# Second attention: scores from a head's own 32 rows, two heads side by side in the array, in place of zero-padded key copies

## The chip, the core and the metric

One core of one Trainium2 chip runs the whole program. The metric is the device time of one execution in microseconds; three runs of a kernel are taken and the median counts. Lower is better.

## The reference

Input `x` has 8 batches of 256 positions and 512 channels. What matters here is the second attention, over each batch's 256 channels-as-positions with 16 heads of 32 columns:

```python
q, k, v = (proj(Wq), proj(Wk), proj(Wv))          # 16 heads, d = 32
q, k = _rope(q, k, s, d, hidden_states.dtype)
scores = einsum('bhqd,bhkd->bhqk', q, k) / sqrt(d)
scores = maximum(scores + causal, neg)
tmp_sum = sum(softmax(scores), axis=-2)           # column sums
_, topk_idx = top_k(tmp_sum, heavy_budget)        # 25 of 256 columns
scores = where(heavy_mask | band, scores, neg)
attn = einsum('bhqk,bhkd->bhqd', softmax(scores), v) @ Wo.T
x = x + attn
x = x + ffn(gru(cond, x))
...
```

A first attention comes before it, a recurrent network and a mixture of experts behind it; neither is touched.

## The kernel before

The program is written engine by engine: each of PE (matrix products), ACT (activation functions), DVE (vector operations), POOL (general processor) and SP (transfers) has a hand-written order, and semaphores tie them together. `second_attention` runs eight batches one after the other. Queries and keys lie transposed: `rot[:, 0]` holds the rotated queries and `rot[:, 1]` the rotated keys, 128 partitions by 4 groups by 256 positions, so that four heads of 32 rows share a group of partitions. For head h, `m = h // 4` is the group and `q = h % 4` its place in it, so its rows are 32q to 32q + 31.

Before, the keys of the four places were copied into `kz[:, q]` with all rows but those of place q set to zero (a product with the 0/1 column `C_HEAD + q`): q = 0 and 1 by ACT (line 679), q = 2 and 3 by DVE (line 804). A head's score product then runs over all 128 rows, since the zeros take out the other three heads.

A batch has these stages:

- First round, 16 heads. PE: `scores(b, 0, h)`, two bf16 products that write the causal mask (lines 509, 510) and two f32 score products (line 518, query rows 0 to 127 with 128 keys; line 520, query rows 128 to 255 with 256 keys). Each f32 product runs as two weight loads and two passes. The result of head h lies in PSUM bank h % 4, so PE waits until ACT has read head h - 4. DVE: two maxima per head (lines 776, 777), then the reciprocal of head h - 1 (line 783) and its copy into `rdiag` (line 814). ACT: two exponentials (lines 662, 664). After heads 6, 10, 14 and at the end PE adds up columns for four heads at a time in four 32-column tiles of the array (line 566).
- PE then makes V (line 555) and the next batch's projections (line 528), while DVE picks the heavy columns (lines 824 to 840) and turns them into `lcol` (line 843). POOL makes a diagonal for each head from it (line 449), into `NDG` buffers.
- Second round, 16 heads. PE: `scores(b, 1, h)` with three more mask products (lines 515 to 517) that need head h's diagonal; then three transposes of head h - 3 (line 594), and after heads 7, 11, 15 and at the end the product with V of four heads in four column tiles (lines 610, 613). DVE: maxima as before, then reciprocal and two scalings of head h - 1 (lines 854, 856). ACT: exponentials, a copy of the transposes of head h - 2 (line 698), and every four heads a copy of the output (line 703).
- Seam. PE: rotation products (line 539) and output projection (line 625). DVE: rotation of the next batch (lines 795 to 800), its two copies into `kz` (line 804), then four additions to x1T (line 864). The next first round's scores wait for the copies and for all four additions, because the projection uses the same PSUM banks.

Of the kernel before, what the change touches and what calls it, by code (L numbers as in the profile page):

```python
# [9 lines left out]
ALU = mybir.AluOpType  # L10
ACT = mybir.ActivationFunctionType
AX = mybir.AxisListType

P = 128
B, S, D = 8, 256, 512
KD = D // P
KS = S // P
NH = 16
DH1 = S // NH
DH2 = D // NH  # L20
HPC = P // DH2
# [25 lines left out]
C_HEAD = C_SINK + S  # L47
# [329 lines left out]
def second_attention(nc, ins, ps, cst, ident, x1T, hT, tab, weights, d_qk, d_vo, d_tab, d_xT, gru, sb, sem):  # L377
    st = ExitStack()
    with st:
        wq, wk, wv, wo = weights  # L380
        masks = sb(st, "masks", [P, 4, P], BF16)
        raw = sb(st, "raw", [P, 2, KD, S])
        rot = sb(st, "rot", [P, 2, KD, S])
        kz = sb(st, "kz", [P, HPC, KD, S])
        v = sb(st, "v", [P, KS, D])
        tmp = sb(st, "tmp", [P, KD, S])
        E = sb(st, "E", [P, NEX, P + S])
# [13 lines left out]
        dg = sb(st, "dg", [P, NDG, KS, P], BF16)  # L401
# [13 lines left out]
        a_raw = sem(st, "a_raw")  # L415
        p_rot = sem(st, "p_rot")
        v_rot = sem(st, "v_rot")
        a_kz = sem(st, "a_kz")
        v_kz = sem(st, "v_kz")
        p_v = sem(st, "p_v")  # L420
        a_v = sem(st, "a_v")
        p_s = sem(st, "p_s")
        v_m = sem(st, "v_m")
        a_e = sem(st, "a_e")
# [6 lines left out]
        g_d = sem(st, "g_d")  # L431
# [6 lines left out]
        v_x = sem(st, "v_x")  # L438

        with nc.Block() as block:  # L440
# [43 lines left out]
            def _(pe):  # L484
# [4 lines left out]

                def scores(b, r, h, more=False):  # L490

                    n = b * (2 * NH) + r * NH + h
                    bank = h % 4
                    m, q = h // HPC, h % HPC
                    if r == 0 and h < 4:
                        if h == 0:
                            pe.wait_ge(v_x, b * KD + 1)
                    else:
                        pe.wait_ge(a_e, (n - 4 + 1) * 2)
                    if r == 0 and h == 0:  # L500
                        pe.wait_ge(v_rot, b * 6 + 6)
                    if r == 0 and h < 2:
                        pe.wait_ge(a_kz, b * 2 + h + 2)
                    elif r == 0 and h < HPC:
                        pe.wait_ge(v_kz, b * 2 + h - 1)
                    if r == 1 and h == 0 and more:
                        pe.wait_ge(a_raw, b * 2 + 4)
                    kw = dict(stop=False, skip_group_check=True)
                    nc.tensor.matmul(ps[:, bank, 0:P], masks[:, 0, :], masks[:, 1, :], start=True, **kw)
                    nc.tensor.matmul(ps[:, bank, 2 * P:3 * P], masks[:, 0, :], masks[:, 1, :], start=False, **kw)  # L510
                    if r == 1:

                        pe.wait_ge(g_d, b * NH + h + 1)
                        d = dg[:, h % NDG, :, :]
                        nc.tensor.matmul(ps[:, bank, 0:P], masks[:, 2, :], d[:, 0, :], start=False, **kw)
                        nc.tensor.matmul(ps[:, bank, P:2 * P], masks[:, 3, :], d[:, 0, :], start=False, **kw)
                        nc.tensor.matmul(ps[:, bank, 2 * P:3 * P], masks[:, 2, :], d[:, 1, :], start=False, **kw)
                    nc.tensor.matmul(ps[:, bank, 0:P], rot[:, 0, m, 0:P], kz[:, q, m, 0:P],  # L518
                                     start=False, stop=True, skip_group_check=True)
                    nc.tensor.matmul(ps[:, bank, P:P + S], rot[:, 0, m, P:S], kz[:, q, m, :],  # L520
                                     start=False, stop=True, skip_group_check=True).then_inc(p_s, 1)

                def project(b):

# [19 lines left out]
                def batch(b, more):  # L544

                    for h in range(NH + AHEAD_SUMS):
                        if h < NH:
                            scores(b, 0, h)
                        if h == NH:

                            if b == 0:
                                pe.wait_ge(d_vo, 32)
                            for c in range(KS):
                                for k in range(KD):
                                    last = nc.tensor.matmul(ps[:, 6 + c, :], hT[:, k, b, c * P:(c + 1) * P], wv[:, k, :],
                                                            start=(k == 0), stop=(k == KD - 1))
                            last.then_inc(p_v, 1)
                        g = h - AHEAD_SUMS
                        if g >= 0 and g % CGS == CGS - 1:

                            g0 = g - CGS + 1
                            pe.wait_ge(v_d, b * NH + g + 1)
                            for part, (e0, e1) in enumerate(((0, P), (P, P + S))):
                                for g in range(g0, g0 + CGS):
                                    rows = (g % CGS) * CG
                                    last = nc.tensor.matmul(ps[rows:rows + CG, 4, 0:e1 - e0], rdiag[:, g, part, :],
                                                            E[:, g % NEX, e0:e1], start=(g0 == 0 and part == 0),
                                                            stop=(g0 + CGS == NH and part == 1),
                                                            tile_position=(0, rows), skip_group_check=True)
                            last.then_inc(p_c, 1)  # L570
# [4 lines left out]
                    for c in range(KS):  # L575
                        last = nc.tensor.matmul(ps[:, 5, c * P:(c + 1) * P], light[:, c * P:(c + 1) * P],
                                                ident, start=True, stop=True)
                    last.then_inc(p_l, 1)

                    for h in range(NH + AHEAD + 1):  # L580
                        if h < NH:
                            scores(b, 1, h, more)
                        g = h - AHEAD
                        if 0 <= g < NH:
# [62 lines left out]
            def _(act):  # L647
# [16 lines left out]
                    nc.scalar.activation(E[:, h % NEX, P:P + S], ps[:, bank, P:P + S], ACT.Exp,  # L664
                                         bias=nm[:, r, h, 1:2], accum_out=ls[:, r, h, 1:2]).then_inc(a_e, 1)

                act.nop().then_inc(a_kz, 1)
                act.wait_ge(d_tab, 16)
                def copy_raw(b):
                    for i in range(2):  # L670
# [3 lines left out]
                                             ACT.Copy).then_inc(a_raw, 1)  # L674

                def batch(b, more):
                    act.wait_ge(v_rot, b * 6 + 6)
                    for q in range(2):
                        nc.scalar.activation(kz[:, q, :, :].rearrange("p m s -> p (m s)"),
                                             rot[:, 1, :, :].rearrange("p m s -> p (m s)"), ACT.Copy,  # L680
                                             scale=tab[:, C_HEAD + q:C_HEAD + q + 1]).then_inc(a_kz, 1)
                    for h in range(NH):
                        exps(b, 0, h)
                    act.wait_ge(p_v, b + 2)
# [28 lines left out]
            def _(dve):  # L713
# [72 lines left out]
                def rotate(b):  # L786

                    for i, (c, s) in enumerate(((C_COSQ, C_SINQ), (C_COSK, C_SINK))):
                        dve.wait_ge(p_rot, b * 2 + i + 1)
                        if i == 0:  # L790
                            dve.wait_ge(p_s, b * 2 * NH + 1)
                            dve.wait_ge(a_kz, b * 2 + 1)
                        cos = tab[:, c:c + S].unsqueeze(1).broadcast_to((P, KD, S))
                        sin = tab[:, s:s + S].unsqueeze(1).broadcast_to((P, KD, S))
                        nc.vector.tensor_tensor(tmp[:, :, :],
# [4 lines left out]
                        nc.vector.tensor_tensor(rot[:, i, :, :], rot[:, i, :, :], tmp[:, :, :], ALU.add)\  # L800
                            .then_inc(v_rot, 1)
                        dve.wait_ge(v_rot, b * 6 + 3 * i + 3)
                    for q in range(2, HPC):
                        nc.vector.tensor_scalar(kz[:, q, :, :], rot[:, 1, :, :], tab[:, C_HEAD + q:C_HEAD + q + 1],
                                                None, ALU.mult).then_inc(v_kz, 1)

                def batch(b, more):
                    for h in range(NH + 1):
# [76 lines left out]
    return (h % CGS) * CG + h // CGS  # L885


NDG = 3
K_STEPS = 2 + 2 * (HEAVY // 8) + 5 * (HEAVY % 8)


# [877 lines left out]
```

## Time and profile before

| what | before |
|---|---|
| median of three runs (range) | 2164.16 us (2162.59 to 2166.87) |
| profiled execution, its time | 2168.39 us |
| its span, first to last instruction | 2166.6 us |
| mean granted PE clock | 0.957 |
| PE busy | 1972.8 us (91%) |
| PE weight loads busy | 1693.5 us (78%) |
| DVE busy | 1381.9 us (64%) |
| ACT busy | 897.6 us (41%) |
| POOL busy | 318.5 us (15%) |

The profile is of one execution; the busy shares are means over stages with different limits, and the largest group of all, line 1048 of the recurrent network, lies after the second attention. A stage is read from the table of stretches (busy time of each engine between two moments) and from the timeline (instructions of one engine in order of time, with the idle time before one and the instruction that ended it). Matrix products overlap in the array: the time that each shows includes its way through the array, so the pitch from one start to the next is the cost.

### The profile page before, as it was taken

What the parts mean: (1) busy time and instruction counts of PE and PEld (TensorE: products, weight loads), DVE (VectorE), ACT (ScalarE), POOL (GpSimd) and SP (SyncE); (2) the same over time, 40 slices, a digit from 0 to 9 for tenths busy, and PEclk for the clock granted to TensorE, in tenths of its full rate; (3) what the DMA queues carried; (4) which work ended last, traced back from release to release, by engine and by line L of the source; (5) the groups of instructions that cost most, each with busy time, mean ns of one, the idle gap of its engine ahead of it and who ended that gap; (6) DMA issues with size and microseconds to landing.
All of it is one profiled execution on the core that took longest, in us unless ns stands there. A gap on an engine that the chain in (4) does not pass through costs nothing.

```text
span 2166.6 us, 80653 instructions
## 1 busy us (share of the span) xinstructions
PE 1972.8 (91%) x34348; PEld 1693.5 (78%) x34348; DVE 1381.9 (64%) x5702; ACT 897.6 (41%) x2894; POOL 318.5 (15%) x471
## 2 busy tenths in 40 slices
PE   5899999999998999886899999998998998999999
PEld 3677677677676889775798898897887987988988
DVE  5565666666666155677677677677676775776763
ACT  1355455455455233343343343343443433433433
POOL 0041231242111000241110110110110100100112
PEclk9999999999999999997999999899999998998999
DMA  8000000000001611111000000000000000000000
GB/s 316 1 1 1 1 1 1 1 1 1 1 1 59 216 61 52 51 45 34 3 18 18 21 11 18 27 4 28 18 5 25 18 18 13 18 18 12 4 12 11
DMA packets 53594, 63.19 MB, mean 29 GB/s; under 512 B 7377, under 2 KB 44113, under 8 KB 52209
## 3 DMA queue, kind: packets, MB, share of 16 engines
q1 hardware_dynamic: 53232, 58.02, 7.9%
q8 instruction: 270, 4.42, 0.9%
q14 instruction: 92, 0.75, 0.1%
HBM read 42.77 MB, written 15.24 MB: 27 GB/s over the span
## 4 chain that ended last, share of the span: by engine, by line
PE 41%; DVE 9%; issue 2%; ACT 1%; DVEq 0%; ACTq 0%
PE ps L1048 22%; PE ps L1492 9%; PE ps L1470 8%; DVE hp L1122 2%; ACT nn L1063 1%; DVE dh L1111 1%; DVE dh L1117 1%; DVE hn L1101 1%; DVE hn L1103 1%; DVE hn L1095 1%; DVE hn L1098 1%; PE ps L1481 1%; DVE hp L1125 1%; DVE ns L1113 1%; DVE h L1123 0%
## 5 line engine op out<-in xcount | busy, mean ns | idle before, releaser
L1048 PEld LDWEIGHTS ps<-hp,whf 128*128 128x128 f16 x24576 | 644.7, 96 | 111.7 <-DVE hp L1125 89.9
L1048 PE MATMUL ps<-hp,whf 128*128 128x32 f16 x24576 | 660.3, 177 | 73.4 <-DVE hp L1125 67.5
L1063 ACT ACTIVATE rz<-s,sc 128x32 f32<-128x32 f32 x512 | 164.6, 322 | 402.9 <-DVE s L1092 395.6
L1470 PE MATMUL ps<-hs,w1f 128*128 128x256 f16 x2112 | 285.4, 281 | 34.5 <-DVE wi L1671 34.5
L1492 PE MATMUL ps<-wi,w2f 128*128 128x256 f16 x2112 | 276.5, 279 | 0.0
L1591 POOL TENSOR_TENSOR wi<-wi 128x256 f16<-128x256 f32 x176 | 120.4, 689 | 1035.7 <-ACT wi L1571 1035.7
L1470 PEld LDWEIGHTS ps<-hs,w1f 128*128 128x128 f16 x2112 | 208.7, 101 | 72.3 <-DVE wi L1671 40.4
L1492 PEld LDWEIGHTS ps<-wi,w2f 128*128 128x128 f16 x2112 | 195.3, 99 | 27.2 <-issue 3.0
L1090 DVE TENSOR_TENSOR s<-ps,gi 128x32 f32<-128x32 f32 x256 | 48.6, 190 | 232.4 <-PE ps L1048 232.0
L1063 ACT ACTIVATE nn<-hn,sc 128x32 f32<-128x32 f32 x256 | 82.3, 322 | 240.8 <-DVE hn L1103 240.8
L1222 PE MATMUL ps<-x1T,wi 128*128 128x256 f32 x768 | 179.3, 391 | 1.0 <-PEq L440 1.0
L1222 PEld LDWEIGHTS ps<-x1T,wi 128*128 128x128 f32 x768 | 147.4, 196 | 20.9 <-issue 1.4
L520 PE MATMUL ps<-kz,rot 128*128 128x256 f32 x512 | 157.8, 391 | 0.0
L449 POOL TENSOR_TENSOR dg<-masks,lcol 128x256 bf16<-128x256 bf16 x128 | 78.1, 616 | 533.0 <-DVE lcol L843 454.2
L662 ACT ACTIVATE E<-ps,nm 128x128 f32<-128x128 f32 x256 | 94.4, 369 | 80.6 <-DVE nm L777 74.3
L1077 ACT ACTIVATE hs<-hp 128x64 f16<-128x64 f16 x256 | 65.0, 254 | 135.1 <-DVE hp L1125 134.7
L664 ACT ACTIVATE E<-ps,nm 128x256 f32<-128x256 f32 x256 | 120.3, 470 | 0.0
L528 PE MATMUL ps<-hT,wi 128*128 128x256 f32 x512 | 114.7, 385 | 4.8 <-PEq L273 4.8
L518 PE MATMUL ps<-kz,rot 128*128 128x128 f32 x512 | 115.8, 309 | 0.0
L528 PEld LDWEIGHTS ps<-hT,wi 128*128 128x128 f32 x512 | 98.1, 193 | 21.2 <-issue 7.7
L776 DVE TENSOR_REDUCE nm<-ps 128x1 f32<-128x128 f32 x256 | 73.3, 286 | 52.7 <-PE ps L520 50.4
L777 DVE TENSOR_REDUCE nm<-ps 128x1 f32<-128x256 f32 x256 | 105.6, 412 | 0.0
(213 smaller groups left out, 3002.5 us busy)
## 6 DMA issues: line engine op xcount, KB each, us to landing
gi_d<-stage SPq DMA_DIRECT2D x84, 128.0 KB, 1.7
gi<-gi_d SPq DMA_DIRECT2D x14, 768.0 KB, 5.1
w1f<-in_w1T SPq DMA_DIRECT2D x4, 1408.0 KB, 10.3
xall<-in_x SPq DMA_DIRECT2D x4, 1024.0 KB, 9.3
x1T<-in_xT SPq DMA_DIRECT2D x1, 4096.0 KB, 16.1
w2f<-in_w2T SPq DMA_DIRECT2D x16, 256.0 KB, 3.3
out<-x1T SPq DMA_DIRECT2D x8, 512.0 KB, 2.9
whf<-in_W_hh SPq DMA_DIRECT2D x1, 3072.0 KB, 22.4
```

What stands on the lines that cost most here:

```text
L518: nc.tensor.matmul(ps[:, bank, 0:P], rot[:, 0, m, 0:P], kz[:, q, m, 0:P], start=False, stop=True, skip_group_check=True)
L520: nc.tensor.matmul(ps[:, bank, P:P + S], rot[:, 0, m, P:S], kz[:, q, m, :], start=False, stop=True, skip_group_check=True).then_inc(p_s, 1)
L528: last = nc.tensor.matmul(ps[:, 2 * i + m // 2, (m % 2) * S:(m % 2 + 1) * S], w[:, k, m * P:(m + 1) * P], hT[:, k, bass.ds(b, 1), :].rearr ...
L662: nc.scalar.activation(E[:, h % NEX, 0:P], ps[:, bank, 0:P], ACT.Exp, bias=nm[:, r, h, 0:1], accum_out=ls[:, r, h, 0:1]).then_inc(a_e, 1)
L664: nc.scalar.activation(E[:, h % NEX, P:P + S], ps[:, bank, P:P + S], ACT.Exp, bias=nm[:, r, h, 1:2], accum_out=ls[:, r, h, 1:2]).then_inc( ...
L777: nc.vector.tensor_reduce(nm[:, r, h, 1:2], ps[:, bank, P:P + S], AX.X, ALU.max, negate=True).then_inc(v_m, 1)
L1048: last = nc.tensor.matmul(ps[:, bank, g * WIDE * 2 * B:(g + 1) * WIDE * 2 * B], w[:, k, q, g, a, :], moving, start=(k == 0 and a == 0), st ...
L1063: nc.scalar.activation(o.rearrange("p g b -> p (g b)"), i_.rearrange("p g b -> p (g b)"), func, scale=un).then_inc(done, 1)
L1222: last = nc.tensor.matmul(ps[:, bank_of(u), 0:TT], wi[:, k, q * P:(q + 1) * P], x1T[:, k, tile * SPT:(tile + 1) * SPT, :] .rearrange("p s ...
L1470: last = nc.tensor.matmul(ps[:, 6 + i % 2, 0:TT], w1p[:, k, i // NC2, wp, (i % NC2) * P:(i % NC2 + 1) * P], hs[:, f % 2, k, hq, :, :].rear ...
L1492: last = nc.tensor.matmul(ps[:, 4 + m // 2, (m % 2) * TT:(m % 2 + 1) * TT], w2p[:, i // 2, wp, o:o + P], hh[:, j % RING, hq, :], start=Fal ...
L1591: nc.gpsimd.tensor_tensor(hh[:, j % RING, 1, :], tb[:, j % TB, :], hh[:, j % RING, 0, :], ALU.subtract).then_inc(g_l, 1)
```

## The change

`kz` and its copies on ACT and DVE go, with their semaphores. `scores` is now called for even heads alone and handles the pair h, h + 1. For both heads it first waits for their banks and writes the masks (and, in the second round, waits for both diagonals). Then come four products, of 32 rows each and placed at rows 0 and 32, or 64 and 96, of the array by `tile_position`: the first part of h, the first part of h + 1, the second part of h, the second part of h + 1. `p_s` is raised at the second part of each head, hence for both at the end of the pair. The diagonals have four buffers in place of three. Whatever else PE does between heads keeps its place in the loop over h.

```diff
--- before.py
+++ after.py
@@ -381,7 +381,6 @@
         masks = sb(st, "masks", [P, 4, P], BF16)
         raw = sb(st, "raw", [P, 2, KD, S])
         rot = sb(st, "rot", [P, 2, KD, S])
-        kz = sb(st, "kz", [P, HPC, KD, S])
         v = sb(st, "v", [P, KS, D])
         tmp = sb(st, "tmp", [P, KD, S])
         E = sb(st, "E", [P, NEX, P + S])
@@ -415,8 +414,6 @@
         a_raw = sem(st, "a_raw")
         p_rot = sem(st, "p_rot")
         v_rot = sem(st, "v_rot")
-        a_kz = sem(st, "a_kz")
-        v_kz = sem(st, "v_kz")
         p_v = sem(st, "p_v")
         a_v = sem(st, "a_v")
         p_s = sem(st, "p_s")
@@ -489,36 +486,36 @@
 
                 def scores(b, r, h, more=False):
 
-                    n = b * (2 * NH) + r * NH + h
-                    bank = h % 4
-                    m, q = h // HPC, h % HPC
-                    if r == 0 and h < 4:
-                        if h == 0:
-                            pe.wait_ge(v_x, b * KD + 1)
-                    else:
-                        pe.wait_ge(a_e, (n - 4 + 1) * 2)
-                    if r == 0 and h == 0:
-                        pe.wait_ge(v_rot, b * 6 + 6)
-                    if r == 0 and h < 2:
-                        pe.wait_ge(a_kz, b * 2 + h + 2)
-                    elif r == 0 and h < HPC:
-                        pe.wait_ge(v_kz, b * 2 + h - 1)
-                    if r == 1 and h == 0 and more:
-                        pe.wait_ge(a_raw, b * 2 + 4)
-                    kw = dict(stop=False, skip_group_check=True)
-                    nc.tensor.matmul(ps[:, bank, 0:P], masks[:, 0, :], masks[:, 1, :], start=True, **kw)
-                    nc.tensor.matmul(ps[:, bank, 2 * P:3 * P], masks[:, 0, :], masks[:, 1, :], start=False, **kw)
-                    if r == 1:
-
-                        pe.wait_ge(g_d, b * NH + h + 1)
-                        d = dg[:, h % NDG, :, :]
-                        nc.tensor.matmul(ps[:, bank, 0:P], masks[:, 2, :], d[:, 0, :], start=False, **kw)
-                        nc.tensor.matmul(ps[:, bank, P:2 * P], masks[:, 3, :], d[:, 0, :], start=False, **kw)
-                        nc.tensor.matmul(ps[:, bank, 2 * P:3 * P], masks[:, 2, :], d[:, 1, :], start=False, **kw)
-                    nc.tensor.matmul(ps[:, bank, 0:P], rot[:, 0, m, 0:P], kz[:, q, m, 0:P],
-                                     start=False, stop=True, skip_group_check=True)
-                    nc.tensor.matmul(ps[:, bank, P:P + S], rot[:, 0, m, P:S], kz[:, q, m, :],
-                                     start=False, stop=True, skip_group_check=True).then_inc(p_s, 1)
+                    for g in (h, h + 1):
+                        n = b * (2 * NH) + r * NH + g
+                        if r == 0 and g < 4:
+                            if g == 0:
+                                pe.wait_ge(v_x, b * KD + 1)
+                                pe.wait_ge(v_rot, b * 6 + 6)
+                        else:
+                            pe.wait_ge(a_e, (n - 4 + 1) * 2)
+                        if r == 1 and g == 0 and more:
+                            pe.wait_ge(a_raw, b * 2 + 4)
+                        kw = dict(stop=False, skip_group_check=True)
+                        bank = g % 4
+                        nc.tensor.matmul(ps[:, bank, 0:P], masks[:, 0, :], masks[:, 1, :], start=True, **kw)
+                        nc.tensor.matmul(ps[:, bank, 2 * P:3 * P], masks[:, 0, :], masks[:, 1, :], start=False, **kw)
+                        if r == 1:
+
+                            pe.wait_ge(g_d, b * NH + g + 1)
+                            d = dg[:, g % NDG, :, :]
+                            nc.tensor.matmul(ps[:, bank, 0:P], masks[:, 2, :], d[:, 0, :], start=False, **kw)
+                            nc.tensor.matmul(ps[:, bank, P:2 * P], masks[:, 3, :], d[:, 0, :], start=False, **kw)
+                            nc.tensor.matmul(ps[:, bank, 2 * P:3 * P], masks[:, 2, :], d[:, 1, :], start=False, **kw)
+                    for part, (o0, o1, q0, k1) in enumerate(((0, P, 0, P), (P, P + S, P, S))):
+                        for g in (h, h + 1):
+                            m, q = g // HPC, g % HPC
+                            r0 = q * DH2
+                            last = nc.tensor.matmul(ps[:, g % 4, o0:o1], rot[r0:r0 + DH2, 0, m, q0:q0 + P],
+                                                    rot[r0:r0 + DH2, 1, m, 0:k1], start=False, stop=True,
+                                                    tile_position=(r0, 0), skip_group_check=True)
+                            if part == 1:
+                                last.then_inc(p_s, 1)
 
                 def project(b):
 
@@ -544,7 +541,7 @@
                 def batch(b, more):
 
                     for h in range(NH + AHEAD_SUMS):
-                        if h < NH:
+                        if h < NH and h % 2 == 0:
                             scores(b, 0, h)
                         if h == NH:
 
@@ -578,7 +575,7 @@
                     last.then_inc(p_l, 1)
 
                     for h in range(NH + AHEAD + 1):
-                        if h < NH:
+                        if h < NH and h % 2 == 0:
                             scores(b, 1, h, more)
                         g = h - AHEAD
                         if 0 <= g < NH:
@@ -664,7 +661,6 @@
                     nc.scalar.activation(E[:, h % NEX, P:P + S], ps[:, bank, P:P + S], ACT.Exp,
                                          bias=nm[:, r, h, 1:2], accum_out=ls[:, r, h, 1:2]).then_inc(a_e, 1)
 
-                act.nop().then_inc(a_kz, 1)
                 act.wait_ge(d_tab, 16)
                 def copy_raw(b):
                     for i in range(2):
@@ -674,11 +670,6 @@
                                              ACT.Copy).then_inc(a_raw, 1)
 
                 def batch(b, more):
-                    act.wait_ge(v_rot, b * 6 + 6)
-                    for q in range(2):
-                        nc.scalar.activation(kz[:, q, :, :].rearrange("p m s -> p (m s)"),
-                                             rot[:, 1, :, :].rearrange("p m s -> p (m s)"), ACT.Copy,
-                                             scale=tab[:, C_HEAD + q:C_HEAD + q + 1]).then_inc(a_kz, 1)
                     for h in range(NH):
                         exps(b, 0, h)
                     act.wait_ge(p_v, b + 2)
@@ -789,7 +780,6 @@
                         dve.wait_ge(p_rot, b * 2 + i + 1)
                         if i == 0:
                             dve.wait_ge(p_s, b * 2 * NH + 1)
-                            dve.wait_ge(a_kz, b * 2 + 1)
                         cos = tab[:, c:c + S].unsqueeze(1).broadcast_to((P, KD, S))
                         sin = tab[:, s:s + S].unsqueeze(1).broadcast_to((P, KD, S))
                         nc.vector.tensor_tensor(tmp[:, :, :],
@@ -800,9 +790,6 @@
                         nc.vector.tensor_tensor(rot[:, i, :, :], rot[:, i, :, :], tmp[:, :, :], ALU.add)\
                             .then_inc(v_rot, 1)
                         dve.wait_ge(v_rot, b * 6 + 3 * i + 3)
-                    for q in range(2, HPC):
-                        nc.vector.tensor_scalar(kz[:, q, :, :], rot[:, 1, :, :], tab[:, C_HEAD + q:C_HEAD + q + 1],
-                                                None, ALU.mult).then_inc(v_kz, 1)
 
                 def batch(b, more):
                     for h in range(NH + 1):
@@ -885,7 +872,7 @@
     return (h % CGS) * CG + h // CGS
 
 
-NDG = 3
+NDG = 4
 K_STEPS = 2 + 2 * (HEAVY // 8) + 5 * (HEAVY % 8)
```

## Rows read from the trace of the kernel before

**Rows 1.** Table of stretches, third batch: start:end length, busy us (instructions) by engine, clock, DMA.

```profile
239.07:254.90 15.83, 15.83 (x144) 11.85 (x145) 12.46 (x58) 12.78 (x59) 0.00 (x0) 1.00 0.01 2
...
277.96:306.40 28.44, 26.14 (x257) 21.04 (x258) 21.12 (x80) 21.45 (x84) 17.51 (x34) 0.99 0.01 2
```

**Rows 2.** Timeline at the seam before that batch: start us, us, engine, line, operation.

```profile
233.84 2.97 PE L625 MATMUL ps<-oT,wo 128*128 128x256 f32 x13
...
235.51 2.19 ACT L679 ACTIVATE kz<-rot,tab 128x1024 f32<-128x1024 f32 x2 [8.78 <-DVE rot L800]
235.51 1.42 DVE L804 TENSOR_SCALAR kz<-rot,tab 128x1024 f32<-128x1024 f32 x2
236.84 2.17 DVE L864 TENSOR_TENSOR x1T<-ps,x1T 128x256 f32<-128x256 f32 x4
...
239.07 0.23 PE L509 MATMUL ps<-masks 128*128 128x128 bf16 x1 [2.26 <-DVE x1T L864]
```

**Rows 3.** Timeline of PE in its first round, and at the round's end.

```profile
248.20 0.22 PE L509 MATMUL ps<-masks 128*128 128x128 bf16 x1
...
248.31 0.44 PE L518 MATMUL ps<-kz,rot 128*128 128x128 f32 x2
248.59 0.60 PE L520 MATMUL ps<-kz,rot 128*128 128x256 f32 x2
249.12 0.86 PE L566 MATMUL ps<-E,rdiag 128*32 128x128 f32 x16
249.91 0.23 PE L509 MATMUL ps<-masks 128*128 128x128 bf16 x1
...
254.93 0.59 PE L555 MATMUL ps<-wi,hT 128*128 128x512 f32 x1
```

**Rows 4.** Timeline of DVE in the same round: its first maximum, then heads later.

```profile
240.11 0.29 DVE L776 TENSOR_REDUCE nm<-ps 128x1 f32<-128x128 f32 x1 [1.09 <-PE ps L520]
...
248.36 0.17 DVE L783 RECIPROCAL rl<-ls 128x2 f32<-128x2 f32 x1
...
248.63 0.28 DVE L776 TENSOR_REDUCE nm<-ps 128x1 f32<-128x128 f32 x1
...
249.19 0.17 DVE L783 RECIPROCAL rl<-ls 128x2 f32<-128x2 f32 x1
```

**Rows 5.** Timeline of ACT there.

```profile
248.24 0.37 ACT L662 ACTIVATE E<-ps,nm 128x128 f32<-128x128 f32 x1
...
249.28 0.37 ACT L662 ACTIVATE E<-ps,nm 128x128 f32<-128x128 f32 x1
```

**Rows 6.** Timeline of PE in the second round of that batch.

```profile
286.68 0.22 PE L509 MATMUL ps<-masks 128*128 128x128 bf16 x1
...
287.67 0.49 PE L594 MATMUL ps<-cst,En 128*128 128x128 f32 x3
288.15 0.66 PE L610 MATMUL ps<-ET,v 128*32 128x256 f32 x8
...
288.97 0.23 PE L509 MATMUL ps<-masks 128*128 128x128 bf16 x1
```

**Rows 7.** Timeline of ACT there.

```profile
286.81 0.37 ACT L662 ACTIVATE E<-ps,nm 128x128 f32<-128x128 f32 x1
...
287.62 0.49 ACT L698 ACTIVATE ET<-ps 128x384 f32<-128x384 f32 x1
288.12 0.37 ACT L662 ACTIVATE E<-ps,nm 128x128 f32<-128x128 f32 x1
...
290.88 0.38 ACT L703 ACTIVATE oT<-ps 128x256 f32<-128x256 f32 x1
```

**Rows 8.** Timeline of DVE: the first maximum of that round.

```profile
279.50 0.29 DVE L776 TENSOR_REDUCE nm<-ps 128x1 f32<-128x128 f32 x1 [1.84 <-PE ps L520]
```

**Rows 9.** Timeline of POOL: the first four diagonals of that round.

```profile
277.74 2.42 POOL L449 TENSOR_TENSOR dg<-masks,lcol 128x256 bf16<-128x256 bf16 x4 [45.63 <-DVE lcol L843]
```

**Rows 10.** Table of stretches, a stretch of the second batch's first round.

```profile
159.20:162.62 3.42, 3.42 (x14) 2.52 (x13) 1.93 (x9) 2.42 (x11) 0.00 (x0) 0.50 0.00 0
```

## The prediction

> **What bounds the kernel now.** The change touches only the second attention, which runs from about 74 to 713 us of the span, eight batches of some 80 us; what follows it reads its result and moves with its end. So I read the stretches of one batch without a clock drop (the third), first with the table of stretches [rows 1], then the timelines of each engine inside them. A batch has two rounds of 16 heads: scores on PE, row maxima on DVE, exponentials on ACT, with four PSUM banks between them.
>
> In the first round PE is busy without a gap: 15.83 of 15.83 us [rows 1], from the first mask product at 239.07 [rows 2] to the V projection at 254.93 [rows 3], that is 15.86 us. A head costs PE 0.82: two mask products of 0.055 each (248.20 to 248.31), the first score product 0.28 (to 248.59), the second 0.435. After heads 6, 10 and 14 come column sums in column tiles. The second score product starts at 248.59 and would be through at 249.025; the sums start at 249.12, so entering the tiled form costs 0.095. They hold PE for 0.79 until the next mask at 249.91 [rows 3]: sixteen instructions, four heads, both parts, in little more than one head's 0.71. Column tiles thus do run side by side here.
>
> But PE is not far ahead of the others. DVE and ACT form a loop of their own: reciprocal of head h to maximum of h+2 is 0.27 (248.36 to 248.63), maximum to exponential 0.65 (248.63 to 249.28), exponential to its reciprocal 0.95 (248.24 to 249.19) [rows 4, 5]. That is 1.87 per two heads, whatever PE does; PE needs 1.64 and, with its share of the sums, 2.08. **So what PE saves is worth only the small rest above 1.87.**
>
> In the second round a head costs PE 0.99 (286.68 to 287.67, three more masks) and 0.33 of transposes, 1.32; four heads and the 0.97 that the product with V takes (287.67 to 288.97 less the transposes) make 6.25 [rows 6]. ACT needs as much per head: exponentials 0.81 (286.81 to 287.62) and a copy of 0.50 (to 288.12), 1.31 [rows 7]. The round is balanced: a faster PE alone moves little.
>
> At the seam between batches the order is DVE's: rotation, two masked key copies, four additions to x1T, then the scores [rows 2].
>
> **The change part by part.**
>
> *Key copies (kz) go.* DVE's two copies start at 235.51 and its additions at 236.84: 1.33 on the path, since the scores wait for all four additions (idle 2.26 "<-DVE x1T L864") [rows 2]. Late next is the output projection: its last matmuls end at 236.81, while the fourth addition would now start about 237.13 (three of 0.54 after 235.51), so DVE keeps the end and 1.33 is saved whole. ACT's two copies, 2.19 from 235.51, end at 237.70, before the scores start: nothing. Batch 0 has no additions, but waits for ACT's first copy, about 1.1. Sum: 7 x 1.33 + 1.1 = 10.4 saved. The semaphores go for nothing.
>
> *A pair's products.* No row shows row tiles. Bounds: four products in the time of one head's, 0.71 (the column tiles above, nearest), or one after the other, 1.42. I take 0.71, because the tiles of a pair use different rows and banks, as the column tiles use different columns. To it come 0.095 to enter the tiled form, as at the sums, and 0.14 to leave it (0.79 less 0.65, the four passes of one tile at 0.435 per 256 columns): 0.94. A pair in the first round takes 4 x 0.055 + 0.94 = 1.16 against 1.64, in the second 10 x 0.055 + 0.94 = 1.49 against 1.98.
>
> The Trainium skill says, in "TensorEngine Tiling (Array Packing)", Key Properties, that changing the tiling mode drains TensorE. By that rule, the trace agrees at the sums (0.095 and 0.14), and the change meets this switch 128 times where it had none. The skill's "TensorE: Matmul & The Clock Gate", Part 3, gives 3.07x for four row tiles; no run here shows it yet, and with it a pair's block would be an estimated 0.93 rather than 0.71.
>
> *First round.* The first maximum now waits for the pair: 0.22 + 0.095 + 0.71, and 0.22 from product to maximum (1.04 now, 239.07 to 240.11, less 0.82) [rows 2, 4] give 1.25, a loss of 0.2. Then the loop: maximum of head 2 at 1.25 + 0.65 + 0.95 + 0.27 = 3.12, of head 10 four loops later at 10.6, exponentials of 10 and 11 at 11.25 and 12.06, the latter seen done at 13.0. Heads 14 and 15 need the banks of 10 and 11: 0.11 of masks and 0.94, then sums 0.885, so the V projection starts at 14.95 instead of 15.86. I take a gain of 0.85, 6.8 for eight. Bounds: 0.9, and a loss of about 1.75 with products one after the other (a pair 1.16 + 0.71 = 1.87; 8 x 1.87 + 3 x 0.885 = 17.6).
>
> *Second round.* Here pairing costs. The first pair needs two diagonals, and POOL makes four in 2.42 [rows 9]: the second is there at 277.74 + 1.21 = 278.95; with masks, block and release the first maximum comes at 280.14 instead of 279.50 [rows 8], 0.64 late. ACT's early waits absorb some; I take 0.4 at the first V product. A fourth diagonal buffer costs nothing. From one V product to the next a chain closes: product 0.82, the pair 1.49 (a single head's 0.99 now), transposes 0.49, then on ACT copy 0.50, output copy 0.38, exponentials 0.81, copy 0.50, exponentials 0.81, copy 0.50 [rows 6, 7], and some 0.2 of handovers: 6.5, where PE's own 6.25 decides now. That is 0.25 more, and after the second V product the pair again stands where a single head stood, 0.5. Sum 1.15, taken as 1.2, 9.6 for eight. Bounds: 0 (PE has 1 us per four heads to spare and could hide all of it; a gain is excluded by ACT's 1.31 a head) and 0.64 + 3 x 0.5 = 2.15.
>
> *Clock.* PE stands idle 2.26 before each first round; in two rounds with that gap the clock then falls to 0.50 for one stretch (159.20 to 162.62) [rows 10], which costs about 1.7 there. With a gap of 0.9 it may not fall; on the other hand PE will now have gaps inside both rounds. I count nothing, and keep 3 either way for the range.
>
> Sum: -10.4 - 6.8 + 9.6 = -7.6. The profiled execution took 2168.39 (span 2166.60), so 2160.8 by its time; it lies 4.2 above the median of the runs, 2164.16. On the median: **2156.6**.
>
> **Rivals.**
>
> *The row tiles run one after the other (slower).* Place: the block of four products. At 1.42 the first round is PE's again, +1.75; in the second the chain becomes 7.2 (+0.95), with the start about +1.1 and the pair after the V product +1.2, so +3.3. With -1.3 from the copies that is +3.75 a batch, 30: 2194. It decides from the point where the block eats the 0.95 a batch gained: each 0.1 costs 0.1 at three places of the second round and two of the first, so from 0.90. For it: nothing here shows rows side by side. Against: columns do. Chance 0.15.
>
> *The second round pays nothing.* If PE's spare time absorbs the late start and the pairs, -17: 2147. For: PE falls to 5.3 per four heads. Against: the chain above runs through ACT. Chance 0.13.
>
> *Weight loads or the clock.* The loads of a pair do not overlap (each product's first pass waits, 0.28 against 0.22, already now), block 0.9 to 1.0, so 0 to +4; or the clock falls once more in most batches, at 1.7 each, +6 net. 2163 to 2174. For: PE's work falls to 3.2 of 3.74 us in the first round (two pairs and the sums), to 5.3 of 6.5 in the second. Against: the second round has gaps already (26.14 busy of 28.44) and keeps 0.99 [rows 1]. Chance 0.22.
>
> **How the numbers follow.** Forecast 0.50, rivals 0.15, 0.13 and 0.22. The measurement can tell about 0.2%, 4.3 us, from no change. Faster: 0.42 of the forecast and the second rival, 0.55. Within: 0.08 of the forecast and 0.13 of the third, 0.21. Slower: 0.24. The forecast's own range is 2149 to 2163; low takes the second rival with a better clock (2144), high the third (2174); the first, 0.15, and a little below stay out.
>
> **What would show each step.** Right: the additions start at the rotation's end; the pair's four products start within about 0.7, the two row groups within hundredths; first rounds of about 15.0 to the V projection, DVE without gaps; second rounds about 1.2 longer, with ACT or PE waiting after each V product. Wrong: a block of 0.9 or more; a first round still without PE gaps; more stretches at 0.50 in rounds; or a second round as long as before.

## The result, and the profile after

The change makes the kernel slower: 2231.97 us against 2165.51, a ratio of 1.0298 (95% interval 1.0269 to 1.0326). 2156.6 was forecast, with a range of 2144 to 2174.

| what | before | after |
|---|---|---|
| median | 2165.51 us | 2231.97 us |
| profiled execution, span | 2166.6 us | 2222.6 us |
| mean granted PE clock | 0.957 | 0.911 |
| PE busy | 1972.8 us (91%) | 2011.6 us (91%) |
| DVE busy | 1381.9 us (64%) | 1379.2 us (62%) |
| ACT busy | 897.6 us (41%) | 877.1 us (39%) |

Only the clock stands out in such a table, and with it the busy time of PE. The page of the changed kernel shows where it is missing: the second attention runs from the second of the 40 slices to the 14th. Line by line: PE's busy tenths, and the clock granted to it in tenths of full speed.

```profile
PE   6889989999899789978599899999999998999999
...
PEclk9797798787978899989799999999999898999999
```

PE is as busy there as it was, at a lower clock. The seam and a pair look as planned. Timelines of the changed kernel at the seam before the third batch, and of PE and DVE from there (start us, us, engine, line, operation):

```profile
248.65 2.97 PE L622 MATMUL ps<-oT,wo 128*128 128x256 f32 x13
...
250.25 2.18 DVE L851 TENSOR_TENSOR x1T<-ps,x1T 128x256 f32<-128x256 f32 x4
...
252.49 0.23 PE L501 MATMUL ps<-masks 128*128 128x128 bf16 x1 [0.87 <-DVE x1T L851]
```

```profile
252.67 0.22 PE L502 MATMUL ps<-masks 128*128 128x128 bf16 x1
252.82 0.92 PE L514 MATMUL ps<-rot 32*128 32x128 f32 x8
253.67 0.23 PE L501 MATMUL ps<-masks 128*128 128x128 bf16 x1
...
253.77 0.29 DVE L767 TENSOR_REDUCE nm<-ps 128x1 f32<-128x128 f32 x1 [1.34 <-PE ps L514]
...
255.65 0.28 DVE L767 TENSOR_REDUCE nm<-ps 128x1 f32<-128x128 f32 x1
```

The additions start when the rotation ends, and the idle time before the scores falls from 2.26 [rows 2] to 0.87. The eight passes of a pair's four products take 0.85 to the next mask (252.82 to 253.67), what one head's products and the way out of the tiled form were worked out to (0.71 and 0.14); the two row groups do run side by side. The first maximum comes 1.28 after the first mask (1.25 worked out), that of head 2 at 3.16 (3.12).

What follows was not worked out. The same batch in the table of stretches (start:end length, busy us (instructions) of PE, PEld, DVE, ACT, POOL, then the granted clock, DMA share and GB/s):

```profile
252.49:256.60 4.11, 3.12 (x30) 1.90 (x32) 2.31 (x11) 2.02 (x10) 0.00 (x0) 1.00 0.02 6
256.60:272.80 16.20, 16.20 (x117) 8.72 (x116) 10.72 (x50) 10.71 (x51) 0.00 (x0) 0.50 0.00 1
272.80:298.04 25.24, 24.48 (x104) 16.84 (x101) 6.76 (x22) 4.11 (x9) 0.22 (x1) 0.92 0.00 0
298.04:304.40 6.36, 4.59 (x51) 3.20 (x52) 3.58 (x13) 2.36 (x11) 4.49 (x8) 1.00 0.01 3
304.40:314.60 10.20, 10.20 (x68) 7.31 (x70) 6.71 (x25) 6.54 (x27) 2.38 (x4) 0.50 0.00 1
314.60:325.00 10.40, 9.08 (x101) 6.44 (x98) 8.78 (x32) 8.04 (x33) 7.76 (x16) 1.00 0.01 2
```

4.1 us into the first round the clock falls to 0.50 (1.2 GHz in place of 2.4) and stays there to its end, although PE is then busy without a gap, 16.20 of 16.20. It comes back in the V projection, which starts at 272.80. In the second round it falls again for 10 us. Six of the other first rounds look like this, with 16 to 18 us of 20.3 to 20.5 at the low clock; the first batch's, 21.5 us long, is low from its start. The second rounds spend 3 to 14 us each at the low clock. In the profile before, the first batch's first round began with the clock low, those of the second and fifth lost one short stretch [rows 10], and all three came back by themselves.

### The profile page after: what moved, and what is told of

Its sections match the earlier page's. It is cut to its first block, busy times and chain, and to the rows that moved or that the text cites. A ratio compares the mean times of both kernels' runs of the same rounds, so it can differ in the third digit from the quotient of the medians.

```text
span 2222.6 us, 80619 instructions
## 1 busy us (share of the span) xinstructions
PE 2011.6 (91%) x34348; PEld 1665.8 (75%) x34348; DVE 1379.2 (62%) x5686; ACT 877.1 (39%) x2878; POOL 308.6 (14%) x471
## 4 chain that ended last, share of the span: by engine, by line
PE 40%; DVE 9%; issue 2%; ACT 1%; DVEq 0%; ACTq 0%
PE ps L1035 22%; PE ps L1479 9%; PE ps L1457 8%; DVE hp L1109 2%; ACT nn L1050 1%; DVE dh L1098 1%; DVE dh L1104 1%; DVE hn L1088 1%; DVE hn L1090 1%; DVE hn L1082 1%; DVE hn L1085 1%; DVE hp L1112 1%; DVE ns L1100 1%; PE ps L1468 1%; PE ps L1521 0%
## 5 line engine op out<-in xcount | busy, mean ns | idle before, releaser
L514 PE MATMUL ps<-rot 32*128 32x128 f32 (+1 forms) x1024 | 165.1, 456 | 0.0
L514 PEld LDWEIGHTS ps<-rot 32*128 32x128 f32 x1024 | 92.9, 251 | 19.0 <-issue 12.2
## 6 DMA issues: line engine op xcount, KB each, us to landing
w1f<-in_w1T SPq DMA_DIRECT2D x4, 1408.0 KB, 10.4
```

The costliest lines, as they stand in the source:

```text
L514: last = nc.tensor.matmul(ps[:, g % 4, o0:o1], rot[r0:r0 + DH2, 0, m, q0:q0 + P], rot[r0:r0 + DH2, 1, m, 0:k1], start=False, stop=True, ti ...
```

## The experiments

Two theories stood after this. **R**: products on 32 rows let the clock fall, though PE is busy. **G**: the gaps that a faster PE has in the rounds let it fall. A third, **S**, holds the changes into and out of the tiled form responsible.

### Copies alone, one head at a time

The copies and their waits go from the kernel before; the products take the unmasked keys:

```diff
-nc.tensor.matmul(ps[:, bank, 0:P], rot[:, 0, m, 0:P], kz[:, q, m, 0:P], ...
+nc.tensor.matmul(ps[:, bank, 0:P], rot[:, 0, m, 0:P], rot[:, 1, m, 0:P], ...
```

> The order of the kernel before, head by head, with the key copies gone and nothing else changed: each score product runs over all 128 rows of the rotated queries and keys, so it sums four heads (that part of the result is left wrong). It prices the removal of the copies by itself. Every theory: the first rounds start 1.33 us earlier after the rotation, 10.4 us in all, a ratio of 0.995; the granted clock in the attention stays as before (0.97 there) and each first round still holds PE without gaps, 15.9 us to the V projection.

Measured: 2146.99, ratio 0.9917 (0.9887 to 0.9948); the medians of this comparison lie 15.6 us apart. In the profiles the attention ends 10.9 us earlier (702.1 against 713.0); the rest of the difference in span lies behind it, where nothing was changed. So the copies were worth what was forecast for them, 10.4. From the first maximum to the V projection seven batches take 14.82 and the first 15.84; before, five took 14.82 and three 16.5, with part of the round at the low clock. No first round behind a seam falls any more. But in this profile as much low clock lies at seams and in second rounds instead, 31.2 us in the whole attention against 29.0 before; that the shorter wait saves falls is not shown by this run.

### 32 rows without gaps

```diff
+r0 = q * DH2
+for o0, o1, q0, k1 in ((0, P, 0, P), (P, P + S, P, S)):
+    last = nc.tensor.matmul(ps[:, bank, o0:o1], rot[r0:r0 + DH2, 0, m, q0:q0 + P],
+                            rot[r0:r0 + DH2, 1, m, 0:k1], ..., tile_position=(r0, 0))
+last.then_inc(p_s, 1)
```

> Head by head as before, no pairs, key copies gone, but each score product on the head's own 32 rows. PE has no gaps here: a head costs 0.82 + 0.24 for entering and leaving the tiled form, 1.06 in the first round. Theory R (products that use 32 rows of the array lower the granted clock although PE is busy): the clock falls to 0.50 in most of both rounds, a head then costs about 1.9, both rounds grow by some 14 us, in all 2165 + 200 or more. Theory G (the gaps that the faster PE has in the rounds let the clock fall): no gaps, so the clock stays at 1.0, rounds grow by 3.8 us each, less 1.3 at the seam, +50: about 2215 with a clock of 0.97 in the attention.

Measured: 2465.87, ratio 1.139. The third batch's first round in its table of stretches:

```profile
296.66:299.50 2.84, 2.84 (x17) 1.86 (x18) 1.22 (x5) 0.91 (x4) 0.00 (x0) 1.00 0.03 6
299.50:329.14 29.64, 29.64 (x128) 15.49 (x127) 11.47 (x55) 12.80 (x56) 0.00 (x0) 0.50 0.00 1
```

PE has no gap before the fall (2.84 of 2.84) and none behind it, and the clock stays low for the rest of the round. All eight first rounds are low for 27 to 35 us. G can't explain this.

### The changed kernel's gaps with full rows

```diff
+m = h // HPC
+nc.tensor.matmul(ps[:, h % 4, 0:P], rot[:, 0, m, 0:P], rot[:, 1, m, 0:P], ...)
+nc.tensor.matmul(ps[:, h % 4, P:P + S], rot[:, 0, m, P:S], rot[:, 1, m, :], ...).then_inc(p_s, 1)
+nc.tensor.matmul(ps[:, (h + 1) % 4, P:2 * P], rot[:, 0, m, P:S], rot[:, 1, m, 0:P], ...).then_inc(p_s, 1)
```

> The order, waits, buffers and seam of the changed kernel, but products over all 128 rows in the untiled array: for the first head of a pair both parts, for the second head only 128 x 128 of them (the rest of its scores, and the separation of heads, are left out). PE is busy 1.21 us of a pair in the first round (the changed kernel: 1.16 to 1.18) and 1.54 in the second (1.49), so it has the same gaps. Theory G: the clock falls to 0.50 in most of the first rounds as in the changed kernel, time about 2220 to 2230. Theory R: the clock stays near 1.0 in the rounds, first rounds take about 15.0 us to the V projection, second rounds 1 us more than before, time 2155 to 2162.

Measured: 2146.97, ratio 0.9911 (0.9881 to 0.9942). The third batch's first round:

```profile
232.94:247.81 14.87, 12.81 (x128) 9.85 (x128) 11.79 (x57) 12.06 (x56) 0.00 (x0) 1.00 0.01 2
```

PE is idle 14% of the round and the clock stays at 1.00. Gaps of this size do not let it fall, full rows given. G has fallen. The time is 8 us below what R expected here, 2155 to 2162.

### Full rows in the tiled form

One head at a time, the same two changes of form per head as with the 32 rows, four column tiles of 128 rows each:

```diff
+for c0 in range(0, P, DH2):
+    last = nc.tensor.matmul(ps[c0:c0 + DH2, bank, o0:o1], rot[:, 0, m, q0 + c0:q0 + c0 + DH2],
+                            rot[:, 1, m, 0:k1], ..., tile_position=(0, c0))
```

> The counterpart of one_head_32_rows: head by head, no pairs, copies gone, the same two changes of the tiled form per head, but each score product as four column tiles of 128 rows and 32 columns side by side (the rows of all four heads are summed; the separation of heads is left out). Theory R (few rows in use lower the clock): the clock stays near 1.0 in the rounds, a head costs 0.82 + 0.24, first and second rounds 3.8 us longer than before, about 2147 + 61 = 2208. Theory S (changing the tiled form lowers the clock): the clock falls to 0.50 in most of the rounds as with the 32 rows, 2400 or more.

Measured: 2198.15, ratio 1.0145 (1.0118 to 1.0172). The third batch's first round:

```profile
246.59:264.62 18.03, 18.03 (x336) 9.26 (x336) 13.55 (x58) 13.64 (x60) 0.00 (x0) 1.00 0.01 3
```

18.03 against 15.83 [rows 1] is the price of two changes of form for each of 16 heads, some 0.14 a head, and the clock stays at 1.00. S has fallen too, for column tiles; row tiles that change form as often stand in the next run.

### More rows, in the changed kernel itself

The one thing altered is the number of rows of each product:

```diff
-r0 = q * DH2
+r0 = (q % 2) * 2 * DH2
-last = nc.tensor.matmul(ps[:, g % 4, o0:o1], rot[r0:r0 + DH2, 0, m, q0:q0 + P], ...
+last = nc.tensor.matmul(ps[:, g % 4, o0:o1], rot[r0:r0 + 2 * DH2, 0, m, q0:q0 + P], ...
```

> The changed kernel with one thing altered: a pair's products run on 64 rows each, the first head's at rows 0 to 63, the second's at rows 64 to 127 (each sums two heads; the separation of heads is left out). Order, waits, copies, tiled form and its changes, and the side by side of two products are the same, so at full clock it does what the changed kernel was forecast to do. Theory R (few rows in use lower the clock): all 128 rows are in use in a pair, the clock stays near 1.0 in the rounds, first rounds 13.7 to 13.9 us from the first maximum to the V projection, time 2146 to 2158. Theory T (row tiles lower the clock, however many rows they hold): it falls as in the changed kernel, first rounds of 19 us, 2225 to 2232.

Measured: 2149.53, ratio 0.9924 (0.9907 to 0.9941). The third batch, its first 4.11 us by themselves and then stage by stage:

```profile
232.42:236.53 4.11, 3.12 (x30) 1.91 (x32) 2.31 (x11) 2.02 (x10) 0.00 (x0) 1.00 0.02 6
...
232.42:247.35 14.93, 12.61 (x144) 7.13 (x145) 11.69 (x57) 12.02 (x56) 0.00 (x0) 1.00 0.01 2
247.35:270.49 23.14, 22.38 (x105) 16.05 (x101) 7.51 (x26) 4.79 (x11) 0.23 (x1) 1.00 0.00 1
270.49:293.80 23.31, 19.72 (x215) 13.87 (x215) 18.83 (x69) 17.08 (x70) 15.02 (x28) 1.00 0.01 2
```

Same order, same 144 products in the first round, same gaps, same changes into and out of the tiled form: the first 4.11 us hold the same 30 products and the same 3.12 us of PE as in the changed kernel, at 1.00 in both. Then the changed kernel falls to 0.50, and this one stays at 1.00. With 64 rows and 64 rows side by side the clock holds, with 32 and 32 it does not; row tiles as such do not lower it. The difference to the changed kernel, 82 us, is what the clock costs. This run also shows the forecast without it: 2149.5 where 2156.6 was worked out.

One head at a time, as with the 32 rows above, with 64:

```diff
-r0 = q * DH2
+r0 = (q % 2) * 2 * DH2
-    last = nc.tensor.matmul(ps[:, bank, o0:o1], rot[r0:r0 + DH2, 0, m, q0:q0 + P], ...
+    last = nc.tensor.matmul(ps[:, bank, o0:o1], rot[r0:r0 + 2 * DH2, 0, m, q0:q0 + P], ...
```

> As one_head_32_rows, with 64 rows per product (two heads summed). 32 rows gave 2466 with 0.50 in most of the rounds, four column tiles with all 128 rows gave 2198 with none of it, at the same pitch of 1.06 per head. Theory R as a matter of degree: less low time than with 32 rows, 2200 to 2330. If 64 rows are enough, the rounds stay at 1.0 and it takes what the column tiles take, 2195 to 2205; if any row tile lowers the clock, 2440 to 2470.

Measured: 2331.70, ratio 1.076. It lies between. Of its eight first rounds three ran almost wholly at 0.50 and five at 1.00, with the same instructions:

```profile
177.01:209.57 32.56, 32.56 (x144) 17.44 (x145) 12.69 (x58) 13.69 (x60) 0.00 (x0) 0.54 0.00 1
278.43:297.86 19.43, 19.43 (x145) 11.21 (x145) 12.77 (x58) 13.69 (x60) 0.00 (x0) 1.00 0.01 2
```

So with 64 rows the same work ran rounds through at either clock. Low time in the whole attention is 604 us with 32 rows, 290 with 64 and 44 with the column tiles of 128.

Two things changed together in these runs, the rows of one product and the rows in use at a time. With 64 rows to a product, one head at a time (64 in use) falls in three first rounds of eight, and the pairs (128 in use) in none behind the first batch, so the size of a product is not all of it; but the pairs also issue these products in half the time. Four products of 32 rows at once, with all 128 rows in use, would tell the two apart; no run tries that, so which of them counts stays open.

### Filling with full rows

`keep_busy` issues further bf16 mask products of 128 rows:

```diff
 scores(b, 0, h)
+if h not in (6, 10, 14):
+    keep_busy(5, 12)
...
 pe.wait_ge(a_t, n - 1)
+if h < NH and h % 2 == 1:
+    keep_busy(bank, 12)
```

> The changed kernel with 12 extra bf16 products of 128 rows and 128 columns (0.055 us each at full clock, 0.66) per pair, where PE waits anyway: in the first round after pairs that no column sums follow (into a bank not in use), in the second before the transposes of every second head (into their bank, before they write it). Theory G: the gaps are filled, the clock stays at 1.0 almost everywhere, time about 2157 to 2165. Theory R: the full rows raise what PE does, but column sums and row tiles stay: the clock is held in part, time between 2160 and 2200. If neither gaps nor rows matter (for example the clock follows the change of the tiled form), the clock stays as low as in the changed kernel and the time is 2230 or more.

Measured: 2206.91, ratio 1.0196 (1.0156 to 1.0236). It holds the clock at 1.00 in seven of eight first rounds, 13.90 from first maximum to V projection; the first batch, which goes into its round at 0.50, stays there (25.4). The time is 7 us above what R expected. In the second rounds the clock still falls in most batches, and what PE spends on filler comes on top.

With twice the filler in the second round:

```diff
-    keep_busy(bank, 12)
+    keep_busy(bank, 24)
```

> As pairs_with_filler_12, with 24 filler products per pair in the second round in place of 12. There the clock still fell with 12. Theory R: with 24 full-row products per pair the clock holds at 1.0 in the second rounds too (low time in the attention from 140 to below 60 us), but PE then needs 1.49 + 0.66 + 0.49 + 1.32 = 3.96 us per pair where the chain needs 3.25, so rounds of 27 us and a time near 2200. If the row tiles themselves set the clock, whatever runs beside them, it still falls in most second rounds and the time is above 2215.

Measured: 2230.97, one execution. The clock still falls in every second round, so the expectation under R, that it holds, was wrong, and time and falls are those of the other branch, that row tiles set the clock whatever runs beside them. Since the pairs on 64 rows hold it, that can be true of 32 rows alone. The second batch's second round:

```profile
215.40:218.80 3.40, 1.84 (x23) 1.35 (x23) 2.88 (x11) 2.31 (x12) 1.35 (x3) 1.00 0.00 0
218.80:222.20 3.40, 3.40 (x28) 2.69 (x25) 3.17 (x13) 2.39 (x10) 1.19 (x2) 0.51 0.02 5
222.20:236.00 13.80, 13.80 (x197) 11.40 (x195) 8.85 (x32) 8.43 (x32) 5.54 (x10) 1.00 0.01 1
```

Before the fall PE is busy 1.84 of 3.40: filler starts only with the third transposes, and the first ones wait for DVE. Here a gap and few rows come together. The pairs on 64 rows have a gap of 1.47 us at the same place (here 1.56), are busy 1.93 of 3.40 (273.80 to 277.20), and stay at 1.00, so the gap alone does not do it. How gap and rows add up no run here measures.

### Two versions that keep the gain

Copies kept, but off the seam: ACT makes three, DVE the fourth behind its additions.

```diff
-for q in range(2):
+for q in range(3):
     nc.scalar.activation(kz[:, q, :, :]..., rot[:, 1, :, :]..., ACT.Copy, ...)
...
 nc.vector.tensor_tensor(xv, ps[:, m, 0:S], xv, ALU.add).then_inc(v_x, 1)
+if more:
+    last_copy()
```

> The kernel before, whole result, with the key copies kept but taken off the seam: ACT makes three (3.4 us from the end of the rotation, while the additions run), DVE makes the fourth behind its four additions, in the 1.04 us in which it waits for the first scores. If the copies cost time at the seam alone, this gives what their removal gives: the scores start 1.33 us earlier in each batch, 2147 to 2153. If ACT's third copy delays the first exponential or DVE's the first maximum, up to 0.7 us of it per batch is lost: 2153 to 2158.

Measured: 2150.55, ratio 0.9921 (0.9904 to 0.9937): faster than both kernels. Timeline at a seam of it:

```profile
310.79 3.23 ACT L679 ACTIVATE kz<-rot,tab 128x1024 f32<-128x1024 f32 x3 [8.78 <-DVE rot L800]
310.79 2.20 DVE L866 TENSOR_TENSOR x1T<-ps,x1T 128x256 f32<-128x256 f32 x4
312.92 0.73 DVE L806 TENSOR_SCALAR kz<-rot,tab 128x1024 f32<-128x1024 f32 x1
...
313.05 0.23 PE L509 MATMUL ps<-masks 128*128 128x128 bf16 x1 [0.96 <-DVE x1T L866]
```

The additions begin at the rotation's end. DVE's copy fills its wait for the first scores, whose maximum starts at the usual 1.03 after the mask.

Row tiles with filler in the first round alone, one head at a time on full rows in the second, the copies made between the rounds:

```diff
-if h < NH:
-    scores(b, 0, h)
+if h < NH and h % 2 == 0:
+    pair(b, 0, h)
+    if h not in (6, 10, 14):
+        keep_busy(5, 12)
```

> Row tiles where the pairs gained, full rows where they lost: first round as in the changed kernel with 12 filler products per pair (the run with filler kept 1.0 there and took 13.9 us from the first maximum to the V projection, before 14.8), second round head by head over 128 rows as before, with the key copies made between the rounds while ACT and DVE wait for PE. Theory R: clock near 1.0 in both rounds; per batch 1.33 at the seam and 0.9 less 0.2 in the first round gained, 2138 to 2148. If the clock falls in the first rounds again, over 2180.

Measured: 2158.02, ratio 0.9958 (0.9943 to 0.9972). Faster than before, but 10 us short of the expectation, which missed one thing:

```profile
73.21:100.87 27.66, 27.66 (x205) 18.36 (x205) 13.12 (x60) 12.71 (x59) 0.00 (x0) 0.50 0.00 1
164.70:179.87 15.17, 15.17 (x204) 10.46 (x204) 11.95 (x57) 12.04 (x57) 0.00 (x0) 1.00 0.01 2
```

The first batch enters its round with the clock low, and with row tiles in the mix, even PE without a gap doesn't bring it back in that round; against the second batch's round it costs 12.5 us. The other seven hold.

## Why the prediction was wrong, point by point

The step that failed is the paragraph on the clock: "I count nothing, and keep 3 either way for the range". The third rival had the fall in its place ("the clock falls once more in most batches, at 1.7 each"), with a chance of 0.22, but that makes 14 us, and it cost 82. Two things were wrong in it. The price 1.7 was read from a round in which the clock came back by itself [rows 10]; there PE went on with products of 128 rows. In the changed kernel the low clock lasts to the end of the first round. And the argument looked at gaps alone, where rows made the difference. The evidence against, that "the second round has gaps already" and keeps 0.99, was right about gaps, and the full-row run confirms it; it was no evidence about rows, since the eight batches before hold no product of fewer than 128. The first attention of the same trace does hold some, and the prediction does not use them. Timeline of PE before, in the first attention and, for comparison, at the V projection of the third batch:

```profile
6.11 14.02 PE L221 MATMUL ps<-wm,cst 8*128 8x512 f32 x16 [6.11 <-DVE wm L193]
31.13 9.70 PE L231 MATMUL ps<-wv,xwb 128*128 128x256 f32 x32 [11.00 <-DVE xwb L210]
...
254.93 1.88 PE L555 MATMUL ps<-wi,hT 128*128 128x512 f32 x4
```

Sixteen passes on 8 rows follow one another without a gap for 14 us, 0.85 apart, where passes of the same 512 columns on 128 rows come 0.43 apart at 1.00. The 128-row passes of 256 columns behind them begin 0.43 apart and end 0.22 apart. By this pitch the 8 rows ran at the pace of the low clock throughout, with PE busy all the time. The table of stretches prints 1.00 there, so this is a sign from the pitch alone, and no test of rows.

The sums over eight batches say where the time went. First round: first mask to V projection; middle: to the second round's first mask; second round: to the start of its last product with V; seam: to the next first mask, in the last batch to the last projection product. In brackets, us at low clock.

| stage | before | after | after's order, 64 rows |
|---|---|---|---|
| first rounds | 132.6 (12.0) | 164.3 (138.5) | 121.7 (9.3) |
| middle | 176.9 (2.6) | 189.7 (28.4) | 177.7 (3.4) |
| second rounds | 225.0 (7.6) | 251.6 (71.1) | 231.8 (7.0) |
| seam | 102.6 (6.8) | 97.9 (17.1) | 91.2 (3.3) |

After minus the 64 rows is 42.6 + 12.0 + 19.8 + 6.7 = 81 us at the price of the clock, mostly in first rounds.

The other steps, by the 64-row run:

- *Key copies.* Right. An undisturbed seam falls from 13.10 to 11.77, 1.33 as worked out. Not counted were falls of the clock: the profile before has four short ones that this run has not, two in first rounds and two at seams, at 1.7 each.
- *A pair's products.* Right in sum: 0.15 from the last mask's start into the tiled form (0.055 + 0.095), then 0.85 to the next mask. By the starts of the passes that is 0.76 and 0.10 rather than 0.71 and 0.14. The first rival (one after the other) has fallen.
- *First round.* Right: 14.93 to the V projection, 14.95 worked out, 15.86 before. The loop of DVE and ACT sets it: the maxima of heads 2 and 10 come 3.16 and 10.65 after the first mask (3.12 and 10.6 worked out).
- *Second round.* Near in size, 28.72 against 27.72 and 0.1 in the middle, 1.1 lost where 1.2 was forecast; but that is in part luck. The first product with V is 0.79 late, where 0.4 was taken, the second 1.17; from there on nothing more is lost (1.08 and 1.00), where the sum went on from 0.65 to 1.15. The late start was sized too low, and the pair behind the second product with V costs nothing. The second rival (nothing lost) has fallen.
- *Sum.* -1.33 - 0.92 + 1.1 is -1.15 a batch, where -0.95 was forecast, 1.6 us in eight. With the four falls saved (6.7) and one more at the last seam (1.1), that makes up the 7 us by which this run lies below the forecast.

The Trainium skill says in "TensorE: Matmul & The Clock Gate", Part 1, that the gate goes by how busy PE has recently been. The rows differ if that is taken for the profile's busy time: 16.20 of 16.20 us at 0.50 in the changed kernel, 12.61 of 14.93 at 1.00 with 64 rows. Part 3 of the same page of the Trainium skill says that matmuls at different tile positions run concurrently in the array; the trace agrees, with 0.85 for a pair's four products and the way out, where one head's two took 0.71.

## What to carry to other kernels

Before products are put on fewer rows of the array, ask what they do to PE's clock: time per instruction can be right to a hundredth and the stage still run at half speed. Read the granted clock of the stage itself, and what brought it back in the trace at hand; a price read from a fall in one kind of work need not hold in another. If the work at hand holds no products of the new kind, look for some elsewhere in the trace and compare their pitch. When a step is only in the way, moving it into another engine's wait can give all that removing it would give.

## What the runs showed of the hardware

- At equal order and pitch, a pair on 32 + 32 rows ran its first rounds at 0.50 for 138.5 of 164.3 us, on 64 + 64 rows at 1.00, but for part of the first batch's, where the clock was low on entry and came back. One head at a time: 32 rows all first rounds low, 64 rows three of eight, four column tiles of 128 rows none but part of the first batch's, also low on entry.
- On 32 rows a low clock lasted with PE busy: 29.64 us of PE without a gap at 0.50, until full-row projections came. With full-row filler between the row tiles a round entered low stayed low too (27.66 us), and rounds entered high stayed high (15.17).
- Two 32-row products of f32 run side by side: 0.85 for both heads' 384 columns and the way out of the tiled form, where one head's took 0.71 before without it.
- Changing into and out of the tiled form around each head cost a first round 2.2 us (18.03 against 15.83), 0.14 a head.
